# VectorE makes the queries' copy for the odd heads from the second batch on

## What is computed

```
x = x + tanh(g_xattn) * attention(layernorm(x), ctx, ctx, mask)
x = x + tanh(g_ffn)   * experts(layernorm(x))

def attention(query, key, value, mask):      # 16 heads of 16 features, windows of 64 queries
    q = (query @ W_q.T + b_q) / 4;  k = key @ W_k.T + b_k;  v = value @ W_v.T + b_v
    # each window of 64 queries looks at its own and the previous window's keys, causal and masked
    return (softmax(q k^T) v) @ W_o.T + b_o
```

## Time and profile before

| | us |
|---|---|
| median of 3 runs | 324.1 |
| lowest and highest | 322.89, 324.15 |
| the profiled execution | 324.57 |
| its span, first to last instruction | 322.8 |

### The profile page before, as it was taken

How to read it: one execution, slowest core, us unless ns; L and a number is a source line. 1 busy time by engine, 2 the same in 40 slices (tenths; PEclk the granted TensorE clock), 3 DMA queues, 4 the chain that set the end, 5 groups by cost and what they waited for, 6 DMA issues and landing times.

```text
span 322.8 us, 8448 instructions
## 1 busy us (share of the span) xinstructions
PE 299.0 (93%) x2759; PEld 244.6 (76%) x2760; DVE 195.5 (61%) x950; ACT 177.0 (55%) x666; POOL 165.3 (51%) x200
## 2 busy tenths in 40 slices
PE   7868779999999999999897999999999999999994
PEld 3437646887768866777776889898998989898974
DVE  2788898898989879899974232423425161515133
ACT  3379999999999999999754111111110202111110
POOL 6469747789769984989856122131313121121322
PEclk9999999999999999999999999999999999999999
DMA  7921299017512280230324679697979897998900
GB/s 216 288 87 25 61 376 316 7 26 229 197 60 91 58 312 3 87 93 6 95 80 185 164 215 369 201 363 235 367 212 372 238 347 257 306 310 253 365 18 13
DMA packets 48471, 60.55 MB, mean 188 GB/s; under 512 B 14712, under 2 KB 41360, under 8 KB 46384
## 3 DMA queue, kind: packets, MB, share of 16 engines
q1 hardware_dynamic: 44976, 53.20, 51.5%
q0 software_dynamic: 2560, 6.25, 5.3%
q10 hardware_dynamic: 896, 0.61, 0.6%
HBM read 44.60 MB, written 14.19 MB: 182 GB/s over the span
## 4 chain that ended last, share of the span: by engine, by line
PE 58%; ACT 26%; DVE 8%; issue 4%; DMA 1%; POOL 1%; SPq 0%; DVEq 0%; POOLq 0%; ACTq 0%
PE bank L1763 20%; ACT probs L712 18%; PE bank L1788 16%; PE bank L1813 5%; PE bank L1424 3%; ACT probsT L725 3%; DVE probs L958 3%; ACT q_par L686 2%; PE bank L1435 2%; PE bank L1566 1%; DMA x_all<-in_x_dram 1%; PE bank L1774 1%; PE bank L1477 1%; PE bank L1499 1%; PE bank L1537 1%
## 5 line engine op out<-in xcount | busy, mean ns | idle before, releaser
L712 ACT ACTIVATE probs<-probs,low 128x128 f32<-128x128 f32 x256 | 99.4, 407 | 2.2 <-DVE low L958 2.2
L533 POOL TENSOR_TENSOR probs<-probs,r_total 128x512 f32<-128x512 f32 x64 | 66.3, 1046 | 18.1 <-DVE r_total L967 17.6
L1763 PEld LDWEIGHTS bank<-xdT,w 128*128 128x128 f32 x480 | 66.6, 190 | 1.9 <-issue 1.2
L1763 PE MATMUL bank<-xdT,w 128*128 128x160 f32 x480 | 68.0, 300 | 0.0
L958 DVE CUSTOM_DVE_ANT_0 probs<-bank,mask_now 128x128 f32<-128x128 f32 x256 | 57.2, 283 | 6.4 <-PE bank L1465 6.0
L712 ACT ACTIVATION_READ_ACCUMULATOR probs<-probs,low 128x1 f32 x256 | 53.2, 208 | 0.0
L882 ACT ACTIVATE w_raw<-bank 128x480 f32<-128x480 f32 (+1 forms) x24 | 12.4, 526 | 62.7 <-PE bank L1763 35.7
L637 POOL DMA_INDIRECT out_dram<-base,place x16 | 14.0, 874 | 59.2 <-DVE base L1323 37.4
L646 POOL DMA_INDIRECT out_dram<-base,place x16 | 15.7, 979 | 53.7 <-DVE place L1316 43.3
L882 ACT ACTIVATE x_all<-bank 128x480 f32<-128x480 f32 (+1 forms) x24 | 12.6, 526 | 52.2 <-PE bank L1763 32.6
L1333 DVE SCALAR_TENSOR_TENSOR base<-bank,base 128x256 f32<-128x256 f32 x15 | 7.2, 482 | 51.8 <-PE bank L1788 51.8
(11 more groups left out here) (147 smaller groups left out, 494.3 us busy)
## 6 DMA issues: line engine op xcount, KB each, us to landing
w<-in_L_ffn_w_dram SPq DMA_DIRECT2D x32, 1024.0 KB, 8.4
expert_queue<-empty_row SPq DMA_DIRECT2D x1, 5140.0 KB, 17.8
q_blocks<-expert_queue SPq DMA_DIRECT2D x62, 40.0 KB
base<-expert_queue SPq DMA_DIRECT2D x16, 129.0 KB
ctx_rows<-in_ctx_dram SPq DMA_DIRECT2D x4, 512.0 KB, 9.3
out_dram<-rows SPq DMA_DIRECT2D x4, 512.0 KB, 6.3
x_all<-in_x_dram SPq DMA_DIRECT2D x3, 512.0 KB, 7.7
v_shift<-v SPq DMA_DIRECT2D x12, 128.0 KB, 2.3
```

What stands on the lines that cost most here:

```text
L533: pool.tensor_tensor(probs[:, i % NP_], probs[:, i % NP_], r_total[:, i % NP_].unsqueeze(2).to_broadcast([P, PAIRS, 2 * WINDOW]), ALU.mult ...
L712: last = act.activation(probs[:, i % NP_, j], probs[:, i % NP_, j], ACT.Exp, scale=-1.0, bias=low[:, i % NP_, j:j + 1], accum_out=total[:, ...
L1763: last = pe.matmul(ps_hidden[m][:, c * CAP:(c + 1) * CAP], w1_sb[i % 2][:, k, f * P:(f + 1) * P], xdT[i % 2][:, k], start=(k == 0), stop=( ...
```

## The change

From batch 1 on ScalarE makes only the copy for the even heads (e = 0). VectorE makes the one for the odd heads, behind ScalarE's (it waits for `q_taken`) and with the same guard against the scores of the batch before, as one `tensor_scalar` with multiply and add. A new semaphore, `q_odd_taken`, counts these copies. TensorE waits for it where it waited for `q_taken`: in `scores`, before `v_of(b, 0)` and before `k_of(b + 1, 0)`. Batch 0 stays as it was.

```diff
-                for e in range(2):
+                for e in range(2 if n == 0 else 1):
                     last = act.activation(q_par[:, g, :, e, :], ps[:].rearrange("p (w q) -> p w q", q=WINDOW), ACT.Identity,
                                           bias=bias_q[:, e, g:g + 1], scale=scale_q[:, e:e + 1])
                 last.then_inc(q_taken, 1)
...
+            def take_odd_q(n, g, ps):
+                if not 0 < n < B:
+                    return
+                dve.wait_ge(q_taken, value(n, 2, g + 1))
+                dve.wait_ge(scores_ready, value(n - 1, CHUNKS, 3 + g))
+                dve.tensor_scalar(q_par[:, g, :, 1, :], ps[:].rearrange("p (w q) -> p w q", q=WINDOW), scale_q[:, 1:2],
+                                  bias_q[:, 1, g:g + 1], ALU.mult, ALU.add).then_inc(q_odd_taken, 1)
...
                 take_probsT(b - 1, 12)
+                take_odd_q(b, 1, ps_misc)
                 r_total_of(b, 1)
...
                 r_total_of(b, 11)
+                take_odd_q(b + 1, 0, ps_misc)
                 low_of(b, 14)
...
             take_probsT(LAST - 1, 12)
+            take_odd_q(LAST, 1, ps_misc)
             r_total_of(LAST, 1)
...
                 pe.wait_ge(q_taken, value(n, 2, groups))
+                if n > 0:
+                    pe.wait_ge(q_odd_taken, value(n - 1, 2, groups))
                 pe.wait_ge(k_taken, value(n, 2, groups))
...
                 pe.wait_ge(q_taken, value(b, 2, 2))
+                if not first:
+                    pe.wait_ge(q_odd_taken, value(b - 1, 2, 2))
                 v_of(b, 0, ps_misc)
...
                 pe.wait_ge(q_taken, value(b + 1, 2, 1))
+                pe.wait_ge(q_odd_taken, value(b, 2, 1))
                 k_of(b + 1, 0, ps_misc)
...
             pe.wait_ge(q_taken, value(LAST, 2, 2))
+            pe.wait_ge(q_odd_taken, value(LAST - 1, 2, 2))
             v_of(LAST, 0, ps_misc)
```

More of the change, by code:

```diff
@@ L212, in flamingo_kernel @@
         ctxT_ready, ctxT_taken = sem("ctxT_ready"), sem("ctxT_taken")
-        q_ready, q_taken = sem("q_ready"), sem("q_taken")
+        q_ready, q_taken, q_odd_taken = sem("q_ready"), sem("q_taken"), sem("q_odd_taken")
         k_ready, k_taken = sem("k_ready"), sem("k_taken")
```

## The result

The changed kernel takes 327.68 us in the median of four runs (326.0, 326.5, 328.85 and 331.02), before 324.11 us on the same chip. The ratio is 1.0104, with a 95% interval of 1.0056 to 1.0151. Two more measurements of the same kernel, beside the experiments, gave 1.0149 (1.011 to 1.0188) and 1.0099 (1.007 to 1.0129): it is slower by some 1.2%, 2.4 to 4.9 us.

A forecast was written before the change was run, and what follows sets the result against it. The prediction took ScalarE, TensorE and VectorE, tied together with parts of each batch without slack, to bound the attention stage. Terms 1.0 + 0.85 + 0.48 = +2.3 us on the 324.1 us median gave 326.4 us, range 322.9 to 328.3.

The forecast's parts named there:

- Term 1: Batch 1: k_of waits for VectorE's copy, 1.47 us late; scores 1.28 late; +1.0 us at the next pair.
- Term 2: Batch 2: choose 0.63 us late behind VectorE's copy, scores 0.98 late; +0.85 us taken.
- Term 3: Batch 3: low_of of the last batch 0.54 us late, passed on through take_q and exp 4; +0.48 us.
- Group 1's share: Scores start late behind group 1's odd copy: 1.28 us in batch 1, 0.98 us in batch 2.
- The copy's price: Each of VectorE's six 128x512 copies out of PSUM takes 0.65 us, with bounds 0.60 and 0.77.
- The bounds of the whole case: Whole kernel 325.3 to 327.9 us, from TensorE absorbing half or nothing and dearer copies adding at most 0.5.
- A: Attention stage: ScalarE is the bound and the change relieves it; 320.0 us for all 4.1, 322.0 for half; chance 0.15.
- B: Attention stage: lateness dies out in VectorE's idle gaps, gains and losses cancel; 323.6 to 325.2 us; chance 0.22.
- C: Attention stage: lateness adds up whole, at six places; +3.7 us, 327.8 us; chance 0.08.

The follow-up runs named there:

- early: Changed kernel with VectorE making batch 1's group 0 odd copy ahead of x_norm; median 327.6 us, repeated (second spelling) at 326.76 us.
- time_only: Against the kernel before: ScalarE keeps both copies, VectorE gets an unused instruction over constant data at the six places, without new waits; 325.37 us.
- no_odd_copy: Changed kernel without VectorE's odd copies and the waits for them, so from batch 1 on nobody makes the odd copy; 322.54 us.
- again: The changed kernel measured once more, with no edit; 329.08 us, ratio 1.0149.
- g0_only: Changed kernel with only group 0's odd copies on VectorE, those of group 1 staying on ScalarE; 329.77 us, ratio 1.0154.
- warm: Changed kernel with 12 matmuls of zeros on TensorE in the wait before batch 1's k_of; 328.44 us, repeated at 328.46 us.

## Why the prediction was right, and where it was off

**Direction and mechanism** were right: slower, by waits that pass from engine to engine, with ScalarE's relief lost. The median of 327.68 lies 1.3 us above the 326.4 forecast and in the range, and 326.5, the median without the longest run, is 0.1 above it. That closeness is in part luck: the second measurement, 329.08 us, lies above the range's end of 328.3, the trace has lost 3.1 us in the attention stage and not 2.3, and its whole time is only 1.4 above before's because the head and the stretch in front of the experts gave 1.8 back.

**Term 1** (batch 1, +1.0): the trace without a fall of the clock has +0.99. Its steps came as written. k_of was 1.63 us later than its head's lateness allows (1.47 forecast), take_k waited 0.80, take_q 0.50 (57.88 us), and scores came 1.40 late (1.28). The two traces of `early` and `early2`, in which it is gone, show that the handover of group 0 is all of it. What I left out: behind a TensorE wait of 3.2 us in place of 1.5 the granted clock fell in three traces of four (to 0.50 from 48 to 50.5 us), and batch 1 then adds 2.7. The earlier trace rows had the wait, and I worked out how long it would become, but took its cost for its length.

**Term 2** (batch 2, +0.85) was mis-sized, +1.60 measured. Its steps are there: `choose` 0.69 us late (0.63 forecast; 0.98 less 0.31, my own terms, make 0.67), exp_logits late, take_q waiting 1.03 us. Only the wait for the even half isn't: VectorE comes to the copy when that half is out. But `scaled` ended 1.38 late and not 0.63, and with it the ranks, k_of of group 1 and take_q (0.1 forecast); scores started 1.95 late (0.98 forecast), of which 1.60 reached the next batch. The changed kernel's timeline:

```profile
81.33 0.81 DVE L930 TENSOR_SCALAR q_par<-bank,scale_q,bias_q 128x512 f32<-128x512 f32 x1
83.49 1.16 POOL L516 TENSOR_TENSOR mask_next<-key_valid,causal 128x512 bf16<-128x512 bf16 x1
83.55 1.18 DVE L1066 TENSOR_TENSOR scaled<-lowered,rstd 128x64 f32<-128x64 f32 x1
84.76 0.26 ACT L741 ACTIVATE exps<-scaled 128x64 f32<-128x64 f32 x1 [1.45 <-DVE scaled L1066]
95.91 0.78 ACT L686 ACTIVATE q_par<-bank,bias_q,scale_q 128x512 f32<-128x512 f32 x1 [1.03 <-PE bank L1435]
```

`scaled`, an instruction over 64 elements that took 0.21 us in the earlier trace rows, took 1.18: it came to start 0.06 us behind GpSimd's mask instruction and ended 0.08 us behind it. The timeline of before:

```profile
82.05 0.61 POOL L512 CAST key_valid<-mask_u 128x512 bf16<-128x512 uint8 x1
82.25 0.49 DVE L1054 SCALAR_TENSOR_TENSOR marks<-lowered,countdown 128x64 f32<-128x64 f32 x1
82.66 0.21 DVE L1058 TENSOR_TENSOR scaled<-lowered,rstd 128x64 f32<-128x64 f32 x1
82.74 2.27 POOL L516 TENSOR_TENSOR mask_next<-key_valid,causal 128x512 bf16<-128x512 bf16 x2
```

There `scaled` started 0.08 us ahead of the mask instruction and went through, and the instruction before it, `marks`, took 0.49 us beside GpSimd's cast where it takes 0.22 in the changed kernel. The copy's delay thus took one collision of 0.27 us away and brought one of 0.97: 0.69 - 0.27 + 0.97 comes, but for rounding, to the 1.38 measured. So `scaled` ended 0.75 us later than forecast, 0.70 of it by the collisions, and 0.75 us is what term 2 is short of the measured 1.60. `time_only` is the comparison: `choose` starts as late there, and this is its `scaled`, 0.08 us ahead of GpSimd:

```profile
82.59 0.21 DVE L1064 TENSOR_TENSOR scaled<-lowered,rstd 128x64 f32<-128x64 f32 x1
```

The ranks come 0.45 late in it, 0.93 less than in the changed kernel. No run moved GpSimd's instruction alone. That GpSimd's instruction held `scaled` is my reading of these times: 1.18 us from a start 0.06 us behind one of 1.16 us, 0.21 us from a start 0.08 us ahead of it; by what means, no run shows. I had not named GpSimd, and that is what term 2 lacked.

**Term 3** (batch 3, +0.48): +0.53. The copy waited 1.14 and 0.88 us for ScalarE's half, as the prediction had it (0.9 for group 1), and exp 2 waited 0.73 us. `choose` was 0.69 late (0.7 forecast). Take_q, however, was 0.35 late and not 0.54, since `marks` had taken 0.56 us in before and 0.22 after; that the sum fits so well is in part luck.

**Group 1's share** was partly in the wrong place. I charged scores' lateness to the group 1 copy in batches 1 and 2. Alone, it gave -0.25 and +0.51: in batch 1 VectorE reaches it just in time, and ScalarE's 0.68 us come back in part. Of the 0.51, 0.29 was there before the copy ran, as in `no_odd_copy` (`scaled` took 0.63 us), and 0.22 is the copy's. All the larger losses start at group 0.

**The copy's price** was outside my bounds of 0.60 to 0.77: 0.81 us, though the next instruction starts 0.72 us behind it. The bounds of the whole case don't add up either: 0.6 + 0.5 + 0.48 gives 325.7 and not 325.3, and 1.28 + 0.98 + 0.48 with 0.5 for the dearer copies gives 327.3 and not 327.9. Scale and bias from pointers and a result in runs of 64 were a form that no row showed; the nearest row, the plain copy's 0.66 us, was the wrong one.

**The rivals.** A, a gain up to 4.1 us: `no_odd_copy` shows that even the free version of the change gives 1.6 (balance), collisions included; and what was to decide it, the start of the scores of the second chunk, came 1.40 and 1.95 us late in the changed kernel. The copy itself is no gain on VectorE: 0.81 us there, 0.78 on ScalarE. B, that the lateness dies out, held for group 1 and not for group 0. C, +3.7, was nearer in size (measured +3.6 in the first medians), though by other means: it had neither the collision nor the clock, and those are what the traces show beyond the forecast.

## What to carry to other kernels

An engine that is busy 97% of a stage need not be its bound if the others are at 90%: take its work away and see what stands ready to wait (here 4.1 us were worth 1.6). When a step moves from one engine's list to another's, ask first how far the other is in its list at that moment, then what waits behind the step; in batch 1 the same copy cost nothing at group 1 and a full microsecond at group 0, and the place in the list decided it, not its length. Look too at what the delay moves the next short instructions onto, here GpSimd's (1.18 us in place of 0.21 for `scaled`), and at which of them are held already in the kernel before.

## What the runs showed of the hardware

TensorE's granted clock fell from 1.00 to 0.50 behind a wait of 3.2 us in three of four traces (0.50 from 48 to 50.5 us in each, 0.57 over the four microseconds from 47 us in `again`), and behind one of 2.15 us once (0.50 from 92 to 95 us in `g0_only`, 0.61 over the four from 91 us); behind the 2.69 us wait at 24 us, which all kernels share, it fell in ten of the fourteen traces (for example 0.51 from 26 to 28 us in the changed kernel) but not in that of before. With matmuls of zeros in the 3.2 us wait (0.57 us of it left in `warm`) it stayed at 1.00 behind it in both traces. VectorE needs 0.81 us and ScalarE 0.78 for the scaled, biased copy of a 128x512 bank, so between the two there is nothing to gain in this form. And short VectorE instructions that met GpSimd's work on the mask took longer: `scaled` took 1.18 us in place of 0.21 when it started 0.06 us behind a GpSimd instruction of 1.16 us, and 0.21 when it started 0.08 us ahead of it; `mask_now` took 1.40 in place of 0.40 in two traces, and where it took 0.40 in the same place, GpSimd's instruction took 1.45 in place of 1.16.
